# Spreading the gate rows over the partitions: by broadcast DMAs through DRAM in place of TensorE products with a 0/1 matrix

## The reference, cut to what matters

```python
res_hidden = einsum('bsi,ri->bsr', x, A)           # R = 64
logits = einsum('bsi,ei->bse', x, router_w)        # E = 16
probs = softmax(logits)
topw, topi = top_k(probs, 2)
topw = topw / (sum(topw) + 1e-6)
combine = sum(one_hot(topi, 16) * topw[..., None], axis=-2)
delta = einsum('bse,bsr,eor->bso', combine, res_hidden, B)
g = base_out + delta * 0.5
```

## Time and profile before

| | |
|---|---|
| runs (3) | median 699.52 us, 699.08 to 701.77 |
| profiled execution | span 697.0 us from the first to the last instruction; the page gives no time of its own beside it |
| TensorE products (PE) | busy 671.0 us, 96% of the span, 3220 products |
| weight loads (PEld) | 529.0 us, 76% |
| VectorE (DVE) | 457.7 us, 66% |
| ScalarE (ACT) | 208.3 us, 30% |
| GpSimd (POOL) | 204.2 us, 29% |
| SP's DMA queue | 39.90 MB, 17.5% of 16 engines |
| granted TensorE clock | 9 (90% or more of full speed) in all 40 slices |

### The profile page before, as it was taken

One profiled execution on the slowest core, in us unless ns is written; L12 is line 12 of the kernel. 1 busy time (PEld: TensorE's weight loads), 2 busy tenths in 40 slices (PEclk: granted clock), 3 DMA queues, 4 the chain that ended last, 5 costly groups with the idle time before them and its releaser, 6 DMA issues.

```text
span 697.0 us, 9078 instructions
## 1 busy us (share of the span) xinstructions
PE 671.0 (96%) x3220; PEld 529.0 (76%) x3220; DVE 457.7 (66%) x741; ACT 208.3 (30%) x371; POOL 204.2 (29%) x175
## 2 busy tenths in 40 slices
PE   4989999999999999999999999889999999999997
PEld 3867777777777777787777787667877887787787
DVE  8798664596765596665686656684855566485543
ACT  2621222412122312222311132563136115313610
POOL 3299100360000550000630003624424242442441
PEclk9999999999999999999999999999999999999999
DMA  8563000040000040000150004530021013002001
GB/s 273 188 189 111 14 1 0 23 159 0 0 0 0 31 149 0 0 0 0 45 197 1 0 1 122 121 136 1 30 91 62 0 46 135 0 30 90 1 15 46
DMA packets 30570, 40.25 MB, mean 58 GB/s; under 512 B 11888, under 2 KB 12656, under 8 KB 30544
## 3 DMA queue, kind: packets, MB, share of 16 engines
q1 hardware_dynamic: 30544, 39.90, 17.5%
HBM read 31.51 MB, written 8.39 MB: 57 GB/s over the span
## 4 chain that ended last, share of the span: by engine, by line
PE 83%; DVE 9%; issue 4%; DMA 1%; ACT 1%; POOL 1%; SPq 0%; DVEq 0%; POOLq 0%
PE bank L376 73%; DVE eq L916 2%; DVE seg_top L914 2%; PE bank L1201 2%; PE bank L314 2%; DVE counts L926 2%; PE bank L1297 2%; DMA s_tile<-in_L_attn_weight 1%; PE bank L1182 1%; PE bank L1334 1%; PE bank L1162 1%; POOL s_tile L639 1%; DVE h_lo L953 1%; DVE w1T_lo L522 1%; DVE x_tile L354 0%
## 5 line engine op out<-in xcount | busy, mean ns | idle before, releaser
L737 ACT ACTIVATE h_hi<-h 128x512 fp32r<-128x512 f32 x56 | 35.4, 632 | 206.6 <-DVE h L944 206.6
L376 PE MATMUL bank<-w_hi_t,h_hi 128*128 128x512 f32 x224 | 93.6, 418 | 0.8 <-DVE h_lo L953 0.6
L914 DVE TENSOR_REDUCE seg_top<-bank 128x16 f32<-128x512 f32 (+1 forms) x64 | 39.5, 617 | 77.2 <-PE bank L1182 77.2
L376 PE MATMUL bank<-xT_hi,w1T_hi 128*128 128x512 f32 x224 | 88.7, 396 | 0.0
L376 PE MATMUL bank<-w_hi_t,h_lo 128*128 128x512 f32 x224 | 88.5, 395 | 0.0
L376 PE MATMUL bank<-w_lo_t,h_hi 128*128 128x512 f32 x224 | 88.5, 395 | 0.0
L376 PE MATMUL bank<-xT_hi,w1T_lo 128*128 128x512 f32 x224 | 88.5, 395 | 0.0
L376 PE MATMUL bank<-xT_lo,w1T_hi 128*128 128x512 f32 x224 | 88.4, 395 | 0.0
L926 DVE TENSOR_TENSOR_SCAN counts<-restart,eq 128x512 bf16<-128x512 bf16 (+1 forms) x64 | 82.1, 1283 | 2.0
L346 POOL TENSOR_TENSOR rstd<-mean_var,eps 128x4 f32<-128x4 f32 x8 | 1.6, 203 | 271.9 <-DVE mean_var L340 271.9
L360 POOL TENSOR_TENSOR g_tile<-g_tile,s_tile 128x512 f32<-128x512 f32 x31 | 40.6, 1311 | 104.9 <-DVE g_tile L970 66.1
(11 more groups left out here) (201 smaller groups left out, 1327.4 us busy)
## 6 DMA issues: line engine op xcount, KB each, us to landing
x_res<-in_L_attn_data SPq DMA_DIRECT2D x4, 1024.0 KB, 7.6
mid_state<-g_tile SPq DMA_DIRECT2D x16, 256.0 KB, 2.1
x_tile<-mid_state SPq DMA_DIRECT2D x4, 1024.0 KB, 7.5
x_res<-mid_state SPq DMA_DIRECT2D x4, 1024.0 KB, 5.5
out<-g_tile SPq DMA_DIRECT2D x15, 256.0 KB, 2.0
x_tile<-in_L_attn_data SPq DMA_DIRECT2D x3, 1024.0 KB, 5.4
g_tile<-in_L_ffn_w SPq DMA_DIRECT2D x8, 256.0 KB, 5.4
g_tile<-in_L_ffn_w2t SPq DMA_DIRECT2D x8, 256.0 KB, 3.7
```

What stands on the lines that cost most here:

```text
L376: last = nc.tensor.matmul(dst, a, b, start=(start and n == 0), stop=(stop and n == len(mms) - 1))
L737: nc.scalar.activation(h_hi[:, it % 2, :], h[:], ACT.Copy).then_inc(h_hi_done, 1)
L914: nc.vector.reduce_max(seg_top[:, 0:segs], got, AX.X).then_inc(seg_max, 1)
```

## The change

The gates are written once to `comb`, transposed and copied to a `combT` of 16 partitions in float32. SP stores combT to a DRAM tensor `gate_rows` and, when that store has landed and the place is free, issues 16 loads per chunk, each of one gate row of 512 values, broadcast to 64 partitions, into `gate_wide` [128, 8, 512] in SBUF. It lies where `prod_lo` lies, whose part kt is written after prods(kt) has read gate_wide's part kt. `prods` waits for the two loads of its kt and reads gate_wide in place of the bank. The matrix, its construction and the 32 `spread` products go. SP's chunk c = 0 is unrolled. The diff, without the declarations of semaphores and the removal of `def spread`:

```diff
@@ -68,6 +68,7 @@
     mid = nc.dram_tensor("mid_state", (B, S, D), F32, kind="Internal").ap()
     mid_rows = mid.rearrange("b (t p) d -> b p t d", p=P)
+    gates = nc.dram_tensor("gate_rows", (B, E, S), F32, kind="Internal").ap()
     ctx = ExitStack()
     with ctx:
@@ -149,14 +150,13 @@
         base_lo = next_1.take("base_lo", [P, KD, D], F32R)
         wo_hi = next_1.take("wo_hi", [P, D], F32R)
         wo_lo = next_1.take("wo_lo", [P, D], F32R)
-        pick = next_1.take("pick", [2 * Q, KE, P], F32R)
         next_1b = Span(next_1.end)
         base_nat = next_1.take("base_nat", [P, TT, D])
         wo_nat = next_1.take("wo_nat", [P, D])
-        pick_f = next_1.take("pick_f", [2 * Q, KE, P])
         b_nat = next_1.take("b_nat", [P, TT, E, R])
         prod_hi = next_1b.take("prod_hi", [P, KE, S], F32R)
+        gate_wide = nc.alloc_sbuf_tensor_at("gate_wide", [P, KE, S], F32, offset=next_1b.end)
         prod_lo = next_1b.take("prod_lo", [P, KE, S], F32R)
         span_2 = Span(max(span_1.end, next_1.end, next_1b.end))
@@ -185,7 +185,7 @@
         v_lo = rest_2.take("v_lo", [P, TT, DH], F32R)
         at_hi = rest_2.take("at_hi", [P, S], F32R)
         at_lo = rest_2.take("at_lo", [P, S], F32R)
-        combT = rest_2.take("combT", [2 * Q, S], F32R)
+        combT = rest_2.take("combT", [E, S])
         assert max(span_2.end, rest_2.end, before_h.end) <= nc.sbuf_usable_end
...
@@ -596,12 +595,23 @@
             chunk(CH - 1, mid_rows[0], True)
-            def chunk(c, source):
+            def chunk(c, source, first_chunk=False):
                 g = c + CH
                 sp.dma_start(x_res[:], mid_rows[c]).then_inc(ld_res, 16)
                 if source is not None:
                     sp.wait_ge(xT_tr, g * TT + TT)
                     sp.dma_start(x_tile[:], source).then_inc(ld_x, 16)
+                sp.wait_ge(comb_out, c + 1)
+                sp.dma_start(gates[c], combT[:]).then_inc(st_gates, 16)
+                if first_chunk:
+                    sp.wait_ge(w_tr, len(items))
+                else:
+                    sp.wait_ge(y_done, c * TT)
+                sp.wait_ge(st_gates, c * 16 + 16)
+                for e in range(E):
+                    at = slice(e % EPT * R, (e % EPT + 1) * R)
+                    sp.dma_start(gate_wide[at, e // EPT, :], gates[c][e:e + 1, :].to_broadcast([R, S]))\
+                        .then_inc(ld_gates[e // EPT], 16)
                 for tt in range(TT if source is not None else TT - 1):
                     sp.wait_ge(rows_done, g * TT + tt + 1)
                     sp.dma_start(out_rows[c][:, tt, :], g_tile[:, tt, :]).then_inc(st_out, 16)
@@ -615,7 +625,8 @@
                         sp.dma_start(out_rows[c][:, TT - 1, half(i)], g_tile[:, TT - 1, half(i)]).then_inc(st_out, 16)
                     sp.wait_ge(st_out, CH * TT * 16 + 16)
-            with sp.Fori(0, CH - 1) as c:
+            chunk(0, mid_rows[1], True)
+            with sp.Fori(1, CH - 1) as c:
                 chunk(c, mid_rows[c + 1])
             chunk(CH - 1, None)
@@ -657,18 +668,6 @@
             def body(c, last):
                 rows_rstd(gp, c + 1)
-                if last:
-
-
-                    gp.wait_ge(up_done, CH * IT)
-                    gp.memset(pick_f[:], 0.0).then_inc(pick_ready, 1)
-                    for q in range(2):
-                        gp.wait_ge(pick_ready, q + 1)
-                        sq = pick_f[:].rearrange("e k (h r) -> e k h r", r=R)
-                        gp.affine_select(out=sq, in_=sq, compare_op=ALU.not_equal, fill=1.0, base=-q * Q,
-                                         pattern=[[-EPT, KE], [-1, EPT], [0, R]], channel_multiplier=1).then_inc(pick_ready, 1)
-                    gp.wait_ge(pick_ready, 3)
-                    nc.gpsimd.tensor_copy(pick[:], pick_f[:]).then_inc(pick_ready, 1)
                 gp.wait_ge(s_biased, c * TT + TT)
                 for tt in range(TT):
                     gate(gp, c, tt)
@@ -801,7 +800,9 @@
                 for j, src in enumerate((pj[1], sc[0], sc[1])):
                     if j == 2:
                         act.wait_ge(comb_tr, c + 1)
-                        nc.scalar.activation(combT[:], tr[0][0:2 * Q, :], ACT.Copy).then_inc(comb_hi, 1)
+                        if not is_first:
+                            act.wait_ge(st_gates, c * 16)
+                        nc.scalar.activation(combT[:], tr[0][0:E, :], ACT.Copy).then_inc(comb_out, 1)
                     act.wait_ge(proj_done, c * 4 + j + 2)
                     nc.scalar.activation(qkv[:, j, :], src[:], ACT.Identity, bias=bqkv_col[:, j:j + 1]).then_inc(proj_read, 1)
                     if j < 2:
@@ -1025,9 +1026,7 @@
                 step(v.reciprocal(row_a[:], row_a[:]))
                 step(v.scalar_tensor_tensor(top_w[:, 1], top_cnt[:], 1.0, gate_p[:], ALU.is_equal, ALU.mult))
                 step(v.tensor_tensor(top_w[:, 0], top_w[:, 0], top_w[:, 1], ALU.add))
-                for q in range(2):
-                    step(v.scalar_tensor_tensor(comb[:, :, q * Q:q * Q + E], top_w[:, 0], SCALING, wide(row_a),
-                                                ALU.mult, ALU.mult), q == 1)
+                step(v.scalar_tensor_tensor(comb[:, :, 0:E], top_w[:, 0], SCALING, wide(row_a), ALU.mult, ALU.mult))
                 assert steps[0] == NROUTE
             def score_peak(c, tt):
@@ -1038,10 +1037,12 @@
             def prods(c, kt):
-                dve.wait_ge(spread_done, c * KE + kt + 1)
+                if kt == 0:
+                    dve.wait_ge(proj_read, c * 4 + 1)
+                dve.wait_ge(ld_gates[kt], (c + 1) * EPT * 16)
                 if kt >= 3:
                     dve.wait_ge(prod_split, c * KE + kt - 2)
-                nc.vector.tensor_tensor(prod[:, kt % 3, :], pj[kt % 2][:], res[:], ALU.mult).then_inc(prod_done, 1)
+                nc.vector.tensor_tensor(prod[:, kt % 3, :], gate_wide[:, kt, :], res[:], ALU.mult).then_inc(prod_done, 1)
             def probs_lo(c, kt):
                 dve.wait_ge(p_hi_done, c * TT + kt + 1)
@@ -1104,9 +1105,6 @@
                 if is_first:
                     for n in LATE_GROUPS[3]:
                         item_lo(dve, n)
-                dve.wait_ge(comb_hi, c + 1)
-                nc.vector.tensor_tensor(combT[Q:2 * Q, :], tr[0][Q:2 * Q, :], combT[Q:2 * Q, :].bitcast(F32),
-                                        ALU.subtract).then_inc(comb_split, 1)
                 score_peak(c, 0)
                 two_prods(c, 0)
                 dve.wait_ge(v_hi_done, c + 1)
...
@@ -1379,7 +1369,6 @@
                     if is_first:
                         if j == 0:
                             pe.wait_ge(silu_done, CH * TT)
-                            pe.wait_ge(pick_ready, 4)
                         for n in LATE_GROUPS[j]:
                             item_in(pe, n)
                 pe.wait_ge(qk_split, c * 2 + 2)
@@ -1396,25 +1385,16 @@
                     last = nc.tensor.transpose(tr[1][:, rows(tt)], qkv[:, 2, rows(tt)], ident[:])
                 last.then_inc(v_tr, 1)
-                pe.wait_ge(comb_split, c + 1)
-                spread(c, 0)
-                spread(c, 1)
                 scores(c, 1)
                 base(c, 0, 1, KD)
-                spread(c, 2)
-                spread(c, 3)
                 scores(c, 2)
                 scores(c, 3)
                 base(c, 1)
-                spread(c, 4)
-                spread(c, 5)
                 probs_transpose(c, 0)
                 probs_transpose(c, 1)
                 lora(c, 0, 0, 4)
                 probs_transpose(c, 2)
                 probs_transpose(c, 3)
-                spread(c, 6)
-                spread(c, 7)
                 lora(c, 1, 0, 4)
                 pe.wait_ge(p_split, c * TT + TT)
```

More of the change, by code:

```diff
@@ L262, in block_mask_ffn_then_attention_lora_kernel @@
         wo_split = sem("wo_split")
-        pick_ready = sem("pick_ready")
         logits_out = sem("logits_out")
@@ L268, in block_mask_ffn_then_attention_lora_kernel @@
         comb_tr = sem("comb_tr")
-        comb_hi = sem("comb_hi")
-        comb_split = sem("comb_split")
+        comb_out = sem("comb_out")
+        st_gates = sem("st_gates")
+        ld_gates = [sem(f"ld_gates_{kt}") for kt in range(KE)]
         proj_done = sem("proj_done")
@@ L288, in block_mask_ffn_then_attention_lora_kernel @@
         a_split = sem("a_split")
-        spread_done = sem("spread_done")
         prod_done = sem("prod_done")
@@ L400, in block_mask_ffn_then_attention_lora_kernel @@
         tr = [banks[6], banks[7]]
-        NROUTE = 19
+        NROUTE = 18
         EARLY = [banks[i] for i in (2, 3, 4, 5, 7)]
@@ L1289, in scores @@
                     .then_inc(score_done, 1)
[L1291 to L1297, removed]
             def base(c, tt, k0=0, k1=KD):
```

## The result

The changed kernel is slower: 714.5 us median (712.6 to 715.3, four runs) against 700.3 us, a ratio of 1.0196 with an interval of 1.0173 to 1.0218. I had forecast 704.5 us with a range up to 711. The direction was right, the size was not: 14 us in place of 5.

What follows compares the result with a forecast made beforehand. TensorE, busy 96%, was taken to bound the kernel. Matrix -1.7, c = 0 +0.35, c = 1 and 2 +2.65 each, c = 3 +1.1 make +5.05 on 697.0; with 2.5 carried over, 704.5 us, range 697 to 711.

Steps and rivals of the forecast that it cites:

- Part 4: Second-stage chunks: late gates hold peak 1, exp 1 and scores(3); 4.9 us of idle TensorE, net +1.95 us in c = 1.
- a TensorE product counts 0.23 us: Walk of chunk c = 1: each TensorE product takes 0.23 us, since 18 take 4.38 with one restart.
- Part 3: Gate transfers in c = 1: store lands at 526.6, loads 2.25 us after issue, 0.6 us apart; kt = 1 at 530.65.
- part 5: prods with two SBUF operands waits beside GpSimd's prod_lo, making exp 3 late: +2.65 us in c = 1 instead of +1.95.
- Part 1: End of the first stage: without building the 0/1 matrix, x_tile shortens and two TensorE waits go; -1.7 us.
- part 2: Small items: a comb step, the combT subtraction, the combT copy and ScalarE's new store wait; worth 0 on the chain.
- Slow broadcasts: Rival: gate loads take 3.9 us each, 0.7 us apart; 710 us, near 715 with 1 us issues; chance 0.16.
- break-even: Chunk c = 1: kt = 1 landing at about 528.8; each microsecond later costs a microsecond a chunk.
- That prods would not wait for GpSimd: Rival: no lock between prods and GpSimd in the second stage; 700.9 us, chance 0.17.
- Hidden loads: Rival: store not held behind x_tile, loads land 1.7 us after issue; 694.4 us, or 687.2 if no one waits; chance 0.12.
- the second rival: No lock between prods and GpSimd: 700.9 us; chance given as 0.17, with 0.16 of it counted between 696 and 703.

Runs made afterwards that it cites:

- fillers: The changed kernel with 16 unused filler products on TensorE between scores(2) and scores(3), where it waits for exp 1: 709.7 us, ratio 1.0141.
- the first new order: The changed kernel with all four score peaks and exps ahead of the gate waits and TensorE's list reordered to match: 700.7 us, ratio 1.0011.
- the second new order: The changed kernel with peaks and exps ahead of the gate waits, TensorE reordered, and x_tile's load issued behind the gate loads: 700.6 us, ratio 1.0004.

## Why the prediction was wrong

**Part 4 failed, in the term "a TensorE product counts 0.23 us".** I computed a wait of 4.9 us and then let TensorE go on at full speed behind it. The runs show 0.43 us for each product until the clock is back: 5.18, 6.44, 5.76 and 6.09 us for 15 products against 3.48, 9.6 us in the four chunks. About 1.1 us of them are the four restarts, which cost 0.3 us each at full clock too, and 8.4 us are the clock. The 9.6 us are most of the 11.4 us by which the spans differ from my sum; the rest lies mostly in front of c = 0 (0.7 us) and in c = 0, where the second load of kt = 1 landed at 467.80 and not at 466.65. No row of the profile before has TensorE idle for so long in the second stage, its clock was a row of 9s, and I read that as a constant when it was a result of the work. The first stage of that profile has such a row, at its start (TensorE's timeline, four transposes of one line each):

```profile
10.91 1.12 PE L461 MATMUL bank<-ident,g_tile 128*128 128x128 f32 x4 [5.75 <-DMA g_tile<-in_L_ffn_w]
...
26.37 0.60 PE L461 MATMUL bank<-ident,x_res 128*128 128x128 f32 x4
```

Behind 5.75 us of idle time the same number of transposes takes nearly twice as long. The clock column gives 1.00 for both places, so these rows don't show the cause, but they were a reason to put a price on slow products behind a wait.

The Trainium skill's page "TensorE: Matmul & The Clock Gate", part 1, says that the throttled state is the default and that activity releases it. By that rule a change which makes a wait on the busiest engine has to pay for it twice. The windows above agree (1.00, then 0.50 in the wait, 1.00 again after work resumed), and it was a rival that I should have priced.

**Part 3 was right in kind, short in size.** Loads land 2.9 us after their issue, not 2.25, and are 0.65 us apart in the loop, where I took 0.6; the store took 3.2 us, to 3 us forecast. I had the second load of kt = 1 at 530.65 in the frame of c = 1; it is there at 534.34, or 531.8 after subtracting the 2.5 us by which the chunk runs later. The first `prods` of c = 1 starts 6.95 us after combT's copy, where 5.9 was forecast. TensorE's four waits are 5.0, 5.9, 5.5 and 3.9 us, 20.2 in all. The prediction works out one of them, 4.9 us in c = 1, which is a microsecond short; most of that microsecond replaces a loss that I had put elsewhere, see part 5. That the store stands behind x_tile was right: 3.22 against 1.60 us.

**Part 5 was right as a mechanism, and in three chunks did not cost what I took.** prods does wait for GpSimd once both operands are in SBUF (up to 1.8 us, undone by a PSUM operand). As the Trainium skill's page "SBUF — State Buffer" has it, an instruction with one SBUF input stays free of that: all 32 at 676 to 690 ns. But I charged 0.7 us a chunk for exp 3 coming after base(1). At half clock base(1) ended at 543.8, long after exp 3, so this was covered by the larger loss. It became visible only where the wait was gone, in the kernel with early gates. In c = 0 it did cost: there the second `prods` stands in the chain that ended last with 1.80 us, beside a prod_lo, and not with 0.69, some 1.1 us where the prediction had 1.55 (+0.35 against -1.2):

```profile
467.83 1.80 DVE prod L1045
```

**Part 1 was right, part 2 was not tested by itself.** The matrix: -1.7 forecast, 18.84 to 17.12 us measured, and again 17.11 with the matrix only moved. The spreads' 10.6 us and these 1.7 us together, 12.3, are near what the experiments without the long waits win back: 9 us with early gates, where 3.4 us of waits are left, and 10 with prods freed too. Nothing in the runs speaks against the zeros of part 2, but none isolates them.

**The rivals.** Slow broadcasts, 710 us and near 715 with an issue of 1 us each, were nearest by number and wrong by cause: loads land after 2.9 us and not 3.9, and are issued 0.65 us apart. That prods would not wait for GpSimd is refuted by its 1.80 us. Hidden loads were priced at 694 or 687 us; early gates gave 691.5 and 690.0, and a new order with real ones 693.6; the change as made has no such slack, because kt = 1 landed 3 us behind break-even. In the paragraph on how the numbers follow, the second rival stands with 0.16, above with 0.17; this changes nothing.

## What to carry to other kernels

A wait of 4 to 6 us on a TensorE that was busy until then cost its length and then 1.7 to 3.0 us more in slow products (some 3.5 us in the kernel with the late VectorE), so first find cover for it, and only then look at the size of the transfer. When work moves from the busiest engine to a transfer, look in each in-order engine at what stands behind the new wait: here an order with four peaks and exps ahead of it, and TensorE's list to match, gave back 14 us, while fillers or a faster store gave 5 each. Where one engine's operand moves from PSUM to SBUF, check what GpSimd does at the same time.

## What the runs showed of the hardware that I had not expected

- Idle times of 3.9 to 5.9 us brought the granted clock to 0.50 in each of four chunks, and so did 3.1 us behind the fillers; there the clock was still 1.00 when work resumed at 534.3 and fell within the next microsecond. The 1.0 us wait of the earlier trace rows did nothing. The half clock lasted from 3 to 7 us.
- Waits of 1.8 to 2.0 us went either way: 1.8 us behind the fillers in c = 2 and 1.8 us in c = 0 of the first new order lost the clock, while 1.9 us behind the fillers in c = 3, 2.0 us with x_tile behind the gates and all four waits of up to 1.9 us in the second new order kept it.
- The same wait also went either way from one execution to the next, far from the change. In all eleven profiles TensorE waits 1.8 us at about 48 us, in code that no edit touched, and 1.6 to 1.7 us at about 452 us (2.2 us in the two kernels with the copy of res). In six profiles, that of the kernel before among them, the clock stays at 1.00 at both places; in five it is 0.50 for some 3 us behind each. The kernel before, then the one with the matrix built later:

```profile
454.00:455.00 1.00, 1.00 (x7) 0.91 (x8) 0.90 (x6) 0.54 (x2) 0.00 (x0) 1.00 0.00 0
```

```profile
454.00:455.00 1.00, 1.00 (x5) 1.00 (x6) 0.96 (x3) 0.12 (x2) 0.86 (x2) 0.50 0.00 0
```

  In the kernel with early gates the executions with a mean clock of 1.000 have spans of 687.9 and 688.8 us, those with 0.995 have 690.5 and 691.9. So some 3 us between two executions of one kernel can be the clock alone, and the profile with x_tile behind the gates, which holds both losses, may for that reason lie above what was expected.
- The broadcast loads together moved less than the large ones: 168 to 221 GB/s in the microseconds from 531 to 541, with the DMA engines busy for 0.53 to 0.92 of the time, against 359 GB/s with 0.98 while x_res and x_tile were in flight. One load of 128 KB every 0.65 us would be 202 GB/s, an estimate from SP's issues in the chain of c = 1, so the spacing of the issues is enough to explain the rate; whether anything else limits it isn't shown.

```profile
525.00:527.00 2.00, 2.00 (x13) 1.69 (x12) 0.15 (x2) 1.27 (x2) 0.00 (x0) 1.00 0.98 359
```

- In c = 0, where x_res and x_tile were issued just ahead, the 32 KB store took 6.0 us; in c = 3, with nothing left in the queue ahead, 1.59 us.
